# Attention followed by a Mamba-2 layer on one core: the decays between tokens as exponentials of differences, in place of scans

## What is computed

```
h    = group_norm(x);  q, k, v = split(h @ qkv_w.T + qkv_b)
x    = x + softmax(q @ k.T / sqrt(128)) @ v @ proj_w.T + proj_b

u    = layer_norm(x over channels)
z, xBC, dt = split(u @ in_w.T);  dt = softplus(dt + dt_bias)        # 4 heads
xs, B, C   = split(silu(causal_conv(xBC, 4 taps)))
A    = -exp(A_log)
for each token t:                                                   # state: 4 heads x 32 x 64
    state = state * exp(dt[t] * A) + (dt[t] * xs[t]) outer B[t]
    y[t]  = state @ C[t]
y    = rms_norm((y + Dp * xs) * silu(z)) @ out_w.T
out  = x + y * sigmoid(small_mlp(mean(y over tokens)))
```

## Time and profile before

| | us |
|---|---|
| median of 3 runs | 294.8 (294.73 to 295.31) |
| the profiled execution | 295.02 |
| its span in the profile | 292.9 |
| busy PE, DVE, ACT, POOL | 264.2, 239.9, 206.0, 111.3 |

### The profile page before, as it was taken

One profiled execution on the slowest core, in us unless ns is written; L12 is line 12 of the kernel. 1 busy time (PEld: TensorE's weight loads), 2 busy tenths in 40 slices (PEclk: granted clock), 3 DMA queues, 4 the chain that ended last, 5 costly groups with the idle time before them and its releaser, 6 DMA issues.

```text
span 292.9 us, 6133 instructions
## 1 busy us (share of the span) xinstructions
PE 264.2 (90%) x1976; PEld 224.1 (77%) x1976; DVE 239.9 (82%) x520; ACT 206.0 (70%) x406; POOL 111.3 (38%) x114
## 2 busy tenths in 40 slices
PE   3999999999999899999998999998899697878881
PEld 2888898878889689878976987887788595665771
DVE  6777852766678979879999998899999998999943
ACT  2345679887979697879688778876478586767251
POOL 7000115601007815123681343082733728382150
PEclk9999999999999999999999999999999999979796
DMA  6910000000014000082000044040160000000012
GB/s 187 410 63 3 0 3 0 0 2 0 2 54 132 1 0 2 12 229 92 1 2 0 6 143 109 2 144 2 41 215 1 2 37 2 36 0 2 0 40 107
DMA packets 10987, 15.29 MB, mean 52 GB/s; under 512 B 1515, under 2 KB 5708, under 8 KB 10956
## 3 DMA queue, kind: packets, MB, share of 16 engines
q1 hardware_dynamic: 10412, 14.69, 15.7%
q10 hardware_dynamic: 544, 0.21, 0.3%
HBM read 12.70 MB, written 2.20 MB: 51 GB/s over the span
## 4 chain that ended last, share of the span: by engine, by line
PE 56%; DVE 26%; issue 10%; ACT 3%; POOL 2%; DVEq 1%; ACTq 0%; POOLq 0%
PE mamba L1130 17%; PE attn_out L1130 15%; PE scores L1130 13%; PE turn L1203 7%; DVE L L1043 4%; DVE neg_max L948 3%; PE turn L1130 2%; DVE L L1054 2%; DVE scanned L1062 2%; DVE pre L987 2%; DVE th L1082 1%; PE mamba L1266 1%; DVE xdt L1031 1%; DVE th L1074 1%; DVE y L1095 1%
## 5 line engine op out<-in xcount | busy, mean ns | idle before, releaser
L1130 PE MATMUL attn_out<-values,pT 128*128 128x129 f32 x512 | 66.7, 276 | 3.9 <-DVE res L959 3.8
L1130 PEld LDWEIGHTS attn_out<-values,pT 128*128 128x128 f32 x512 | 62.1, 191 | 7.3 <-issue 6.0
L948 DVE TENSOR_REDUCE neg_max<-scores 128x1 f32<-128x1024 f32 x32 | 39.0, 1220 | 15.9 <-PE scores L1130 15.6
L639 ACT ACTIVATE probs<-scores,neg_max 128x512 f32<-128x512 f32 x64 | 42.5, 686 | 12.5 <-DVE neg_max L948 9.8
L645 ACT ACTIVATE pT<-turn 128x512 f32<-128x512 f32 x64 | 37.9, 597 | 15.5 <-PE turn L1203 14.2
L1203 PE MATMUL turn<-ident,probs 128*128 128x128 f32 x256 | 37.8, 274 | 0.3
L1203 PEld LDWEIGHTS turn<-ident,probs 128*128 128x128 f32 x256 | 30.0, 142 | 5.1 <-issue 3.0
L1043 DVE TENSOR_TENSOR_SCAN L<-L,ident 128x512 f32<-128x512 f32 x24 | 30.9, 1302 | 0.0
L1130 PE MATMUL scores<-h_hi,q_hi 128*128 128x512 f32 x64 | 29.7, 465 | 0.2
L1130 PE MATMUL mamba<-u,winC 128*128 128x512 f32 x48 | 24.7, 603 | 1.6 <-DVE y L1095 1.6
L565 POOL TENSOR_TENSOR pre<-pre,th 128x512 f32<-128x512 f32 x16 | 21.6, 1348 | 11.9 <-ACT pre L671 6.9
(11 more groups left out here) (210 smaller groups left out, 605.2 us busy)
## 6 DMA issues: line engine op xcount, KB each, us to landing
L<-decay_rows_d SPq DMA_DIRECT2D x24, 256.0 KB, 3.9
res<-in_x_tok SPq DMA_DIRECT2D x4, 512.0 KB, 8.1
out<-res SPq DMA_DIRECT2D x8, 256.0 KB, 2.2
x_all<-in_x SPq DMA_DIRECT2D x3, 512.0 KB, 8.5
decay_in<-decay_rows_d SPq DMA_DIRECT2D x24, 64.0 KB, 3.3
x_all<-in_x SPq DMA_DIRECT2D x2, 256.0 KB, 3.1
winT<-in_in_wT SPq DMA_DIRECT2D x1, 194.0 KB, 6.9
wqkv<-in_qkv_w ACTq DMA_DIRECT2D x1, 192.0 KB, 4.0
```

The lines of the kernel that those rows point to most:

```text
L639: act.activation(probs[:, i % 2, half_of(h)], scores[:, half_of(h)], ACT.Exp, bias=neg_max[:, i:i + 1]).then_inc(exp_done.sem, 1)
L948: V.tensor_reduce(neg_max[:, n:n + 1], scores[:, :], AX.X, ALU.max, negate=True).then_inc(max_ready.sem, 1)
L1130: return T.matmul(o, w, v, start=start, stop=stop)
```

## The change

`l` isn't a scan any more. `dA` (ACT) now copies the running sums of `la` from the bank of `Cum` instead of taking exp of `la`, so the rows that are spread hold running sums. Then, per chunk, L = exp(sum at i - sum at s), capped at exp(-1000) = 0 below the diagonal:

- a, b, c: `sub` (POOL: 128x512 minus a column per head), `cap` (POOL: `affine_select` over 128x512), `l` (ACT: exp over 128x512), all in place in `L`. That is 24 steps of each kind.
- d: the product `L` becomes three products into one bank (picked rows; minus the sum at s; a large negative number below the diagonal), each 512 columns wide, and `l` (ACT) takes exp from the bank. `dA_T` gets a second copy (`dA_all`). 8 chunks.
- `win_ev` builds `below`, `ident_r`, `row_pick`, `minus_row` (4 small DVE instructions and one wait); `ident4`, `first` and their 5 instructions go.
- `ORDER` is written anew as a whole.

```diff
+                elif kind == "sub":
+                    chunk = L[:, HEADS * n:HEADS * (n + 1), :]
+                    c = n % QUAD
+                    wait(pool, spread[n], b, 16)
+                    wait(pool, dA_ready, b, n // QUAD + 1)
+                    pool.tensor_tensor(chunk, chunk, dA[:, n // QUAD, HEADS * c:HEADS * (c + 1)].unsqueeze(2)
+                                       .broadcast_to([P, HEADS, P]), ALU.subtract).then_inc(sub_ready.sem, 1)
+                elif kind == "cap":
+                    chunk = L[:, HEADS * n:HEADS * (n + 1), :]
+                    wait(pool, sub_ready, b, n + 1)
+                    pool.affine_select(out=chunk, in_=chunk, compare_op=ALU.is_ge, fill=CAP, base=0,
+                                       pattern=[[0, HEADS], [1, P]], channel_multiplier=-1).then_inc(cap_ready.sem, 1)
...
-                    act.activation(dA[:, n, 0:R], la[:, n, :], ACT.Exp, bias=first[:, :], scale=1.0 / A_SCALE
-                                   ).then_inc(dA_ready.sem, 1)
+                    wait(act, sub_ready, b - 1, QUAD * (n + 1))
+                    wait(act, filled["DAT"], b - 1, n + 1)
+                    bank = take(act, b, "Cum", n)
+                    act.activation(dA[:, n, 0:R], bank[:, 0:R], ACT.Copy, scale=1.0 / A_SCALE).then_inc(dA_ready.sem, 1)
...
+                elif kind == "l":
+                    chunk = L[:, HEADS * n:HEADS * (n + 1), :]
+                    if by_dma(b):
+                        wait(act, cap_ready, b, n + 1)
+                        act.activation(chunk, chunk, ACT.Exp).then_inc(l_ready.sem, 1)
+                    else:
+                        wait(act, filled["Y"], b - 1, n // QUAD + 1)
+                        bank = take(act, b, "L", n)
+                        act.activation(chunk, bank[:, :].rearrange("p (h i) -> p h i", h=HEADS), ACT.Exp
+                                       ).then_inc(l_ready.sem, 1)
...
+                    V.tensor_scalar(below[:, :], upto[:, :], 1.0, BELOW, ALU.subtract, ALU.mult)
+                    V.tensor_copy(ident_r[:, :], ident[:, :])
+                    step_done(V.tensor_reduce(row_pick[:, :, :], ident[:, 0:4 * R].rearrange(
+                        "r (s k c h) -> r k c h s", s=2, k=2, c=QUAD)[:, 0], AX.X, ALU.add))
+                    V.tensor_scalar(minus_row[:, :, :], row_pick[:, :, :], -1.0, None, ALU.mult).then_inc(below_ready.sem, 1)
...
                 elif kind == "dA_T":
                     bank = take(dve, b, "DAT", n)
+                    V.tensor_copy(dA_all[:, n, :], bank[:, 0:P]).then_inc(dA_all_ready.sem, 1)
...
-                    V.tensor_tensor_scan(chunk, decays, ident4[:, :, :].rearrange("p a b -> p (a b)"), 0.0, ALU.mult, ALU.add
-                                         ).then_inc(l_ready.sem, 1)
...
                     bank, done = fill(pe, b, "L", QUAD * n + c)
+                    by_head = bank[:, :].rearrange("p (h i) -> p h i", h=HEADS)
                     mm(bank[:, :], pick_chunk[:, c:c + 1].broadcast_to([P, P]),
-                       dA_head[:, n, :, :].rearrange("r h i -> r (h i)")).then_inc(done, 1)
+                       dA_head[:, n, :, :].rearrange("r h i -> r (h i)"), True, False)
+                    mm(by_head, dA_all[:, n, :], minus_row[:, c, :].unsqueeze(2).broadcast_to([P, HEADS, P]), False, False)
+                    mm(by_head, ident_r[:, :], below[:, :].unsqueeze(1).broadcast_to([P, HEADS, P]), False, True
+                       ).then_inc(done, 1)
```

More of the change, by code:

```diff
@@ L116 @@
-conv_bc0d SeA0b@0 T12d@0 yo_dx0c hdn0b T13d@1 conv_bc1d pT12d U1c@2 m4c sp5d m5c SeB0b@0 conv_bc2d sp6d S14d st1c
-tha0b term2d S15d pT13d res5d conv_bc3d sp7d stc1c PV12d max7d PV13d stats5d exp14d sp8d gated0b conv_x0d T14d@0 inv6d
-m6c fin0b Yo1c@2 th_bc0d res6d exp15d m7c Y0c@0 pT14d stats6d store0b yo1c T15d@0 silu0d PV14d pT15d yo_dx1c dA0d c0d
-PV15d y0c gated1b term_x0d g0c Cum0d@1 inv7d res7d cd0d stats7d dec0d sq0c dA_rows0d BT0d@1 ln_ve1d DAT0d@0 Y1c@2 bt0d
-dA_T0d term_x1d ln_pow1d Dec0d@0 y1c L0d@1 conv_x1d u_tok1d l0d L1d@2 decay0d g1c l1d UT1d@0 L2d@1 u1d conv_x2d L3d@2
@@ new lines @@
+raw_bc0d sp3d Pl1b@0 cap5c sp4d term0d T13d@0 inv5d m2c term1d S15d sp5d sub6c res5d l4c InX0d@1 max7d conv_bc0d sub7c
+PV12d pT13d sp6d raw_x0d sp7d pl1b PV13d sp8d m3c conv_bc1d exp14d stats5d Cum0d@0 l5c inv6d XsT1c@1 res6d cd0d cap6c
+SeA0b@2 dA0d T14d@0 dec0d exp15d dA_rows0d Yo0c@0 hdn0b conv_bc2d pT14d T15d@1 xdt1c l6c SeB0b@2 yo0c DAT0d@1 pT15d
+PV14d cap7c dA_T0d term2d PV15d stats6d tha0b yo_dx0c conv_bc3d l7c BT1c@2 G1c@0 to_end1c inv7d bt1c res7d conv_x0d
+xend1c stats7d Dec0d@1 m4c th_bc0d U1c@2 ln_ve1d decay0d silu0d ln_pow1d st1c c0d BT0d@1 bt0d m5c stc1c Y0c@2 gated0b
@@ L130 @@
+store0d store1d
 """.split()
@@ L178, in build @@
         ident = sb("ident", [P, P])
-        ident4 = sb("ident4", [P, HEADS, P])
         center = sb("center", [P, P])
@@ L271, in build @@
         dA_head = sb("dA_head", [P, 2, HEADS, P], F32R)
+        dA_all = sb("dA_all", [P, 2, P], F32R)
+        minus_row, row_pick = sb("minus_row", [P, QUAD, HEADS], F32R), sb("row_pick", [P, QUAD, HEADS])
+        below, ident_r = sb("below", [P, P], F32R), sb("ident_r", [P, P], F32R)
         chunk_decay = sb("chunk_decay", [P, 2, HEADS, HEADDIM, QUAD])
@@ L804, in _ @@
             dve.wait_ge(consts_done.sem, 1)
-            for h in range(HEADS):
-                V.tensor_copy(ident4[:, h, :], ident[:, :])
             V.tensor_scalar(center[:, :], ident[:, :], 1.0 / P, None, ALU.subtract)
```

152 lines of the change are left out of this document (73 added, 79 removed).

## The result

| | before | changed |
|---|---|---|
| median (range), 5 runs each | 294.8 us (294.72 to 295.31) | 292.34 us (291.34 to 292.78) |
| ratio to before, 95% interval | 1 | 0.9907 (0.989 to 0.9924) |
| profiled execution, its span | 295.02, 292.9 | 292.34, 290.6 |

The kernel is 0.9% faster: the sign of the forecast, but 2.5 us where 10.8 were expected, 8.3 us above the point.

The account below looks back on a forecast made before the run. PE was taken to bound A and B, DVE to bound D. Stage terms 15.3 + 36.3 + 51 + 53.5 + 72 + 54 gave a 282.1 us span, 284.0 us against 294.8; likeliest 279 to 289, range 275 to 294.

Parts of the forecast that it names:

- D: Stage from PE step `S0d` to `PV15d`, judged DVE-limited before at 81.3 us; forecast 72 us, PE's 67.5 x 1.07.
- C: Stage from PE step `S0c` to `S0d`, 61.7 us before; forecast 53.5 us, PE's 49.9 x 1.07.
- B: Stage just ahead of C, limited by PE alone, 45.4 us before; forecast 51 us, PE's 49.3 x 1.035.
- The fourth rival: In D, DVE only follows PE, so its relief changes little: D near 79, time 291 to 294 us; chance 0.06.
- POOL's price: 24 `sub` at 1.05 us and 24 `cap` at 1.25 us on POOL: 55 us added, range 38 to 66.
- The lock between DVE and POOL: DVE instructions with two SBUF inputs and POOL additions exclude each other: 9 us added on DVE, 5 in D.
- The tail: Stretch behind D, three parts: forecast 27, 13 and an unchanged 14.1 us, 54 in all.
- The start: Time up to PE step `S0a`: forecast 15.3 us against 15.5 before, 0.2 allowed for the missing copies.
- A: Stage just ahead of B, limited by PE alone: forecast 36.3 us, nothing changes.
- Second rival: POOL becomes the limit in D, which comes to 78 us; time 292 to 293 us; chance 0.15.
- Third rival: `l` in ACT's queue waits for `cap`, delaying attention's `exp` and PE: 16 us over forecast, 299 us; chance 0.13.
- First: Rival: pieces fit better, D at PE's 67.5 x 1.03, C 51.5, tail 51: 275 to 277 us; chance 0.13.

## Why the prediction was right or wrong, point by point

- **What bounds the kernel: right.** D fell from 81.3 to 76.5 and C from 61.7 to 54.3, and B grew by 5.7 as PE's steps said. Of C's 7.4 us, 7.0 are PE's steps that moved away, so C over its PE sum stayed where it was (1.09, before 1.08); that DVE's relief counts there is seen in one and the same order: with scans in it C is 60.8. The fourth rival (DVE a follower in D) gave a time near the measured one, 291 to 294, but by a D of 79, and with POOL's reads reduced D falls further, to 73.7 by its last record (72.8 by the cut of the forecast). The number was right there, not the mechanism.
- **POOL's price: wrong by size, without effect.** `sub` 1.12 (1.05 taken), `cap` 0.685 (1.25 taken, between 0.52 and 1.4: I went to the wrong end). POOL had 151 us, not 170. By POOL's own time this term has about 1.1 us of the result, so the error is harmless there; a longer `cap` would also have read longer.
- **ACT: right.** 220 against 224; `l` 0.63 and 0.60.
- **The lock between DVE and POOL: the step that failed.** "I add 9 us on DVE in all, 5 of them in D" put the waits on DVE and then gave them no time: D was taken as PE x 1.07, as though DVE at 58 had slack and they would vanish in it. The size was near for what `sub` and `cap` do: without their reads the waits fall by 9.2 us, without the two steps by 12.0, and in D DVE's busy time falls from 63.7 to 57.6 (its other work had been put at 53). What was wrong is the path: those reads cost the kernel 5.9 us, 3.7 of them in D. Short steps that wait 0.5 to 1 us stand on the chain there with `neg_max` of the running attention behind them; which single waits make up the 5.9 no run shows. The rows showed the mechanism and I sized it by its share of busy time instead of by who stands behind. With the reads gone, D's 72.8 is near what the sum had (72), and PE is busy for 72.15 of it. Besides, the new order lengthened the waits by some 8 us without `sub` and `cap` (24.0 to 32.0), which no term had. The prediction's own sign of being wrong, means in D that rise by over half a microsecond, came: `dta` 174 to 998 ns, `x_all` 683 to 1221.
- **The tail: under-priced by 2.7.** The first two parts were given 27 + 13 and took 43.8; the last took 12.9, 1.2 less than the 14.1 kept. Exps, products and ACT's queue are ruled out by runs; POOL's reads of d's sums have 1.5 of it by the run without them. I had also left the clock unchanged; in fact it rose, which should have helped. Without that rise the tail would have been longer, by an amount that no run isolates.
- **The start: wrong in the profiled execution.** Minus 0.2 was allowed; it was plus 0.6 in one execution and minus 1.2 in another; why the two differ the records don't show.
- **What is left of the 8.3 us.** Without the reads of `sub` and `cap` the run is at 286.49, 2.5 over the forecast: against its terms that execution has the start +0.8, A -0.3, B -0.7, C -0.9, D +0.8 and the tail about +2.6. So the reads are 5.9 and the tail the rest; of the tail 1.5 has a run behind it and some 1 us stays unexplained, no more than two sets of runs of one kernel differ by (0.9 us).
- **Second rival: refuted.** No POOL stretch is near full (51.1 of 76.5 in D) though its stated time, 292 to 293, is the measured one (its own terms, D 78, B and C 1 more each and the tail 56, add up to 294.0). **Third rival: refuted** by the run without `cap` and by the 1.3 us of waits for it in all 24 `l`. **First: its condition (pieces fit at 1.03) is not reached** even with no POOL work (285.4).
- **The range** held the time; the likeliest case's own (279 to 289) did not. That the range held it is luck: it reached up to 294 for the second rival, a full POOL queue, which did not occur.

## What to carry to other kernels

Work moved to GpSimd is not free because GpSimd is idle: price it by its reading time beside DVE's steps with two SBUF inputs, and look for the short ones at the head of a queue that the critical engine waits for. Look again at what POOL already did, since a new order changes which steps meet. If the work must be there, try giving those short steps an input in PSUM: it cut `dta` from 693 to 174 ns and was worth some 1.3 us, a size that is not settled. And test a rewritten order together with its operations: either half alone was 6 to 8% slower than the kernel before.
